# A two-MoE macaron block on one core: the second scatter and the first picks paced by landings, the second half's routing begun ahead of the first pair

## What is computed

```python
x = x + 0.5 * moe(layernorm(x))
x = x + retention(layernorm(x))       # two layers of retention and FFN, 16 heads
x = x + 0.5 * moe(layernorm(x))

def moe(flat):                        # 4096 tokens x 256
    probs = softmax(flat @ router_w + router_bias)      # 16 experts
    top_w, top_i = top_k(probs, 2)
    norm_w = top_w / (sum(top_w) + 1e-6)
    combine = sum(one_hot(top_i, 16) * norm_w)
    routed = combine[:, 15:16] * flat                   # expert 15 passes the token through
    for e in range(15):
        y = silu(flat @ gate_w[e]) * (flat @ up_w[e]) @ down_w[e]     # 256 -> 128 -> 256
        routed = routed + combine[:, e:e + 1] * y
    shared = silu(causal_conv3(flat, conv_w)) * (flat @ shared_up_w) @ shared_down_w
    return shared + routed
```

## Time and profile before

| | us |
|---|---|
| median of three timed runs | 1405.84 |
| lowest and highest | 1404.09, 1406.28 |
| span of the profiled execution | 1579.5 |

### The profile page before, as it was taken

How to read it: one execution, slowest core, us unless ns; L and a number is a source line. 1 busy time by engine, 2 the same in 40 slices (tenths; PEclk the granted TensorE clock), 3 DMA queues, 4 the chain that set the end, 5 groups by cost and what they waited for, 6 DMA issues and landing times.

```text
span 1579.5 us, 30698 instructions
## 1 busy us (share of the span) xinstructions
PE 1351.4 (86%) x11824; PEld 1104.9 (70%) x11824; DVE 1011.0 (64%) x2391; ACT 614.6 (39%) x1034; POOL 571.9 (36%) x460
## 2 busy tenths in 40 slices
PE   6871968876999999999998999999999676496885
PEld 3461968644788888888886888888887446496753
DVE  5661536658977877777768778797787453253623
ACT  5630635422333433343344334424455262263410
POOL 0726033352342323224424443364343704304252
PEclk9975979989999999999999999999999788698998
DMA  9963559650000000000010000000002463355542
GB/s 326 372 213 122 174 175 321 206 190 23 28 2 2 1 2 1 1 2 32 8 58 1 1 15 2 15 15 14 2 28 89 167 229 131 124 181 171 156 150 90
DMA packets 113867, 151.63 MB, mean 96 GB/s; under 512 B 12224, under 2 KB 96192, under 8 KB 113728
## 3 DMA queue, kind: packets, MB, share of 16 engines
q1 hardware_dynamic: 99328, 114.02, 21.8%
q0 software_dynamic: 12288, 33.57, 6.6%
q10 hardware_dynamic: 2112, 2.10, 0.4%
HBM read 78.21 MB, written 71.43 MB: 95 GB/s over the span
## 4 chain that ended last, share of the span: by engine, by line
PE 53%; DVE 16%; another core or an unknown queue 8%; issue 2%; ACT 2%; POOL 0%; DVEq 0%; ACTq 0%
PE l_w_ps L83 8%; PE l_w_ps L85 7%; PE l_w_ps L84 7%; DVE l_probs L2221 4%; PE l_banks L2505 3%; PE l_rm_ps L2537 2%; PE l_banks L83 2%; PE l_banks L84 2%; PE l_banks L85 2%; DVE l_f_lo L2252 2%; PE l_rm_ps L2530 2%; DVE l_full L2174 1%; PE b_gu_ps L83 1%; PE b_t_ps L1284 1%
## 5 line engine op out<-in xcount | busy, mean ns | idle before, releaser
L2221 DVE TENSOR_TENSOR l_probs<-l_banks,l_past 128x512 f32<-128x512 f32 x256 | 160.1, 684 | 29.8 <-PE l_banks L2505 29.7
L1964 ACT ACTIVATE l_act_f<-l_w_ps,l_ffn_b 128x512 f32<-128x512 f32 x120 | 82.7, 690 | 169.0 <-PE l_w_ps L85 163.9
L83 PE MATMUL l_w_ps<-l_w_hi,l_f_hi 128*128 128x256 f32 x496 | 143.6, 290 | 2.6 <-DVE l_f_lo L2252 2.4
L84 PE MATMUL l_w_ps<-l_w_lo,l_f_hi 128*128 128x256 f32 x496 | 139.6, 281 | 0.0
L85 PE MATMUL l_w_ps<-l_w_hi,l_f_lo 128*128 128x256 f32 x496 | 139.5, 281 | 0.0
L2059 POOL TENSOR_TENSOR l_g_lo<-l_q,l_g_hi 128x1024 fp32r<-128x1024 f32 x16 | 39.1, 2447 | 266.9 <-ACT l_g_hi L1955 266.9
L813 POOL DMA_INDIRECT b_picked<-rows,b_pos_i x64 | 61.1, 955 | 137.4 <-DMA rows<-b_yb 88.5
L83 PE MATMUL l_w_ps<-l_b_hi,l_w_hi 128*128 128x512 f32 x240 | 102.2, 426 | 0.3 <-ACT l_f_hi L1965 0.3
L83 PEld LDWEIGHTS l_w_ps<-l_w_hi,l_f_hi 128*128 128x128 f32 x496 | 93.3, 188 | 8.8 <-issue 8.7
L2252 DVE TENSOR_TENSOR l_f_lo<-l_act_f,l_f_hi 128x512 fp32r<-128x512 f32 x128 | 85.9, 703 | 18.5 <-ACT l_f_hi L1965 18.4
L2046 POOL TENSOR_TENSOR l_q_wide<-l_q,l_pair_mask 128x1024 f32<-128x1024 f32 x32 | 60.1, 1899 | 103.7 <-DVE l_q L2189 100.0
(11 more groups left out here) (432 smaller groups left out, 4053.0 us busy)
## 6 DMA issues: line engine op xcount, KB each, us to landing
rows<-a_zeros SPq DMA_DIRECT2D x14, 1024.0 KB, 10.7
a_xb<-rows SPq DMA_DIRECT2D x46, 256.0 KB
rows<-a_yb SPq DMA_DIRECT2D x46, 256.0 KB
b_xb<-rows SPq DMA_DIRECT2D x46, 256.0 KB
rows<-b_yb SPq DMA_DIRECT2D x46, 256.0 KB
a_w_in<-in_moe_w SPq DMA_DIRECT2D x15, 384.0 KB, 10.2
low_dram<-a_w_lo SPq DMA_DIRECT2D x15, 384.0 KB
b_w_lo<-low_dram SPq DMA_DIRECT2D x15, 384.0 KB
```

The source lines that it names most:

```text
L83: tensor.matmul(out, w_hi, x_hi, start=start, stop=False)
L84: tensor.matmul(out, w_hi, x_lo, start=False, stop=False)
L1964: nc.scalar.activation(act_f[:, f, :], hidden_ps(b, f), ACT.Gelu, bias=ffn1_b[:, b.layer, f:f + 1]).then_inc(act_done, 1)
L2221: dve.tensor_tensor(probs[c % 2][:, r * w:(r + 1) * w].rearrange("p (h n) -> p h n", n=P), banks[:, r, :].rearrange("p (h n) -> p h n", n= ...
```

## The change

It is made in four places, in both MoEs:

- In the second scatter, each transfer but the first waits until the one ahead of it has landed. Transfers of pick 0 and pick 1 alternate, so transfer (c, 0) waits for the c-th landing of `scattered[1][1]`, and (c, 1) for the (c+1)-th of `scattered[1][0]`. The first scatter stays as it was.
- In the picks of the first half, a column's first transfer waits until both transfers of the column ahead have landed.
- VectorE takes one step of `rest()` before `low_x(0)` and one before `low_x(1)`, and two steps instead of one after each of pairs 0 and 1.
- TensorE's `count(1)` stands ahead of the first two `turn_x` instead of inside pair 0.

```diff
@@ scatter(b) @@
                 for c in range(PARTS[b]):
                     for k in range(2):
+                        if b == 1 and (c > 0 or k > 0):
+                            pool.wait_ge(scattered[1][1 - k], 16 * (c + k))
                         pool.indirect_dma_start(own_rows[b], bass.IndirectOffsetOnAxis(ap=pos_i[:, b, k, c:c + 1], axis=0),
                                                 normal(START[b] + c), None).then_inc(scattered[b][k], 16)
@@ pick(c) @@
                 for k in range(2):
+                    if b == 0 and c > 0 and k == 0:
+                        pool.wait_ge(picked_in[(c - 1) % PICKED], 32 * ((c - 1) // PICKED + 1))
@@ vector() @@
                 later = rest()
+            next(later)
             low_x(0)
+            next(later)
             low_x(1)
...
                 low_h(n)
-                next(later, None)
+                for _ in range(2 if n < 2 else 1):
+                    next(later, None)
@@ tensor() @@
+            count(1)
             if begins:
                 pe.wait_ge(dve_lo_done, PIECES)
             turn_x(0)
...
                     turn_x(n + 2)
-                if n == 0:
-                    count(1)
```

## The result

| | timed median, us | runs | profiled span, us |
|---|---|---|---|
| before | 1406.06 | 1404.09 to 1407.06 | 1579.5 |
| changed | 1535.48 | 1530.71 to 1540.30 | 1531.5 |

The changed kernel takes 1.0919 times as long, with an interval of 1.0891 to 1.0948: 129 us more, where 67 had been forecast. The span of its profile is shorter than that of the kernel before, and yet its timed runs are longer. In the changed kernel span and time agree within 4 us; it is the profile of the kernel before that stands apart from its times.

A forecast was written before the change was run, and what follows sets the result against it. TensorE bounds the kernel, pairs at 2.89 us unstalled in timed runs; 31.8 + 33.1 (scatters) - 3.1 (already late) + 2.6 (clock) + 1.9 (routing) + 1 (picks) = 67.3 us on 1405.8 gives 1473.1, range 1415 to 1530.

The forecast's parts named there:

- the landing that sets the scatter's period: Second scatter: 2.57 us from issue to woken waiter, 32 transfers in 82.2 us, 31.8 and 33.1 us late.
- the price of the picks: First half's paced picks: 3.82 us a column, the 16th 1 us late in the first MoE, nothing in the second.
- The sign: Whole kernel, timed against the kernel before: slower 0.86, same 0.04, faster 0.10.
- The scatter's starts: Second scatter, from the earlier routing: start at 103.2 us in the first MoE and 1313.4 in the second.
- The 2.3 us of the prediction's estimate: Second scatter: skill's fixed cost and bandwidth give 2.3 us a transfer, 74 us for 32, time about 1456.
- Rival 4: Second scatter and picks: landings as long as the picks' 3.35 us, from shared DMA engines; 1520 to 1545 us, chance 0.09.
- my upper bound: First half's picks: with a landing of 3.35 us a column takes 4.6 us, the 16th 13 and 7 us late.
- 161 us of stalls: Engine stalls during GpSimd's transfer bursts in the profile before, claimed to belong to the profiled execution, not the timed runs.
- the 174 us: Kernel before: profiled span of 1579.5 us over the timed median of 1405.8, claimed to be nearly all profile stalls.
- Rival 1: Scatter and pick bursts: stalls are in timed runs too and pacing removes them; some 36 us faster, 1370, chance 0.10.
- late in its own scatter: Kernel before, second scatter: 1.7 and 1.4 us late in the two MoEs, together 3.1, subtracted from the forecast's sum.
- The late first pair of the second MoE: Second MoE's start: count ahead of the turns delays the first pair by 1.9 us, bounds 0 and 4.

The follow-up runs named there:

- x1: Kernel before plus only the second scatter's waits, each transfer waiting for the landing of the one ahead, both MoEs: 1511.9 us against 1405.3.
- x5: Changed kernel without its wait in the picks; paced second scatter and early routing kept: 1502.9 us, kernel before 1405.6.
- x7: Changed kernel with SP's queue swapped, each turn's store of y ahead of the load of the pair four ahead: 1531.6 us, kernel before 1405.6.
- x2: Kernel before plus only the waits in the picks of the first half: 1437.5 us against 1405.3.
- x6: Changed kernel with the pick wait made real in the second MoE too, adding the count left by the first: 1565.5 us, kernel before 1405.6.
- x3: Kernel before with only the second half's routing begun early, no new waits: 1407.0 us against 1405.3.
- y1: The changed kernel as it is, on a chip where the kernel before takes 1584.5 us: 1611.8 us, ratio 1.0172.
- x4: Kernel before with each second-scatter transfer waiting for the one two ahead, so two in flight: 1437.4 us against 1405.3.
- x8: Kernel before with each second-scatter transfer waiting for the one three ahead, so three in flight: 1416.7 us against 1405.6.
- z1: Kernel before with two second-scatter transfers in flight and the early routing, no pick waits: 1428.0 us against 1405.8.
- z2: Kernel before with three second-scatter transfers in flight and the early routing: 1407.7 us against 1405.8.
- y2: Kernel before with two second-scatter transfers in flight, on a chip where the kernel before takes 1584.5 us: 1538.4 us, ratio 0.9721.
- x9: Kernel before with the low weight parts' stores moved from SP's turns 28 to 42 to 12 to 26: 1576.6 us against 1578.4.
- x12: Kernel before with the first half's picks waiting for the column two back, both MoEs: 1576.1 us against 1578.4.

## Why the prediction was wrong

The forecast was 1473 us within 1415 to 1530; 1535 were measured. Two terms of the sum carry the miss: the landing that sets the scatter's period, and the price of the picks.

**What held.** The sign, and the mechanism: SP waits for the whole second scatter ahead of pair 23's load, the store of y 16 stands behind it, `take_y(18)` waits, then TensorE starts at half clock. x1 and x5 show that this part costs 106.5 us without the early routing and 97.3 with it, x7 that it is this queue order. The scatter's starts were right within 0.7 us against the first gate of their MoE: 5.2 us behind it where 4.5 was forecast, and 4.1 where 4.7 was.

**Mis-sized: the landing.** I took 2.57 us for a scatter's period, from one landing when no pair ran. Quiet, it is 2.67; beside running pairs 2.6 to 5.1. Means of 3.08 and 2.96 over 31 periods make 15.8 and 12.1 us more: 31.8 forecast and 47.4 measured in the first MoE, 33.1 and 43.3 in the second. The row was from the wrong neighbourhood: nearly half of the 32 transfers lie beside loads and stores of 512 KB a pair, and of the landings shown only the store's 3.24 us was taken there. The 2.3 us of the prediction's estimate is under even the quiet 2.67. Rival 4 had this mechanism, and its range of 1520 to 1545 holds the measured time; I gave it 0.09. That its number fits is in part luck. A period of 3.35 puts 25 us more on each scatter and 19 on the picks; measured were 15.6 and 10.2 more on the scatters and 31 on the picks.

**Mis-sized: the picks.** Forecast 1 us, measured 32.2 (x2). A column takes 5.9 us in the first MoE of x2, not 3.82, nor the 4.6 of my upper bound, since what follows the second issue is 3.2 to 6.3 us and not 2.57. In the prediction's own sum, 16 columns of 5.9 us against 60.2 are 34 us late, so the sum's form was right and the landing in it wrong. Against a pair each of 3.27 the head start of 11 us is used up with the fifth column (the first long pair is 32 to 33). Had the wait been real in the second MoE, it would have cost 30 more (x6).

**Missed: the idle wait.** I read the target of the new wait without asking where the semaphore stood at that time.

**Wrong: where the stalls belong.** I put 161 us of stalls down to the profiled execution. That gave the right base for the timed runs shown, which have no stalls, but by luck, for the reason was wrong: x3's profile is unpaced and free of them, and the timed runs of the kernel before on two chips have them. Spans and times agree within 0.8% in every kernel that I ran. So the 174 us are most simply the difference between two sorts of chips: the profile shown of the kernel before would come from one, its times from the other. That is an inference; on which chip either was taken is not known. The rule that I cited from the Trainium skill (NOTIFIC — the notification-queue block, § 7.1) is not borne out as a cause here: no run shows trace records holding an engine. Rival 1, whose stage is a chip with stalls, fails there too: it promised a gain, and y1 is 27 us slower. It had said itself why: above a period of about 2.9 us the wait costs more than the stall, and y1's is 3.02 in the first MoE.

**Small terms.** The kernel before was not 3.1 us late in its own scatter, but some 0.6. x2 has that scatter on a chip of the first sort; gates 19 to 21 are 6.71 us apart there and 6.12 in x3, where it starts early, and in the second MoE 6.10 and 6.17. The late first pair of the second MoE was forecast at 1.9 us; from the last gate of the first MoE to the first of the second it is 971.3 us on average in the four kernels without the early routing (x1, x2, x4, x8) and 973.8 in the seven with it (changed, x3, x5 to x7, z1, z2), 2.5 more. Together that is +1.9, near the +1.7 of x3 (interval -0.4 to +3.9). The lower clock after a gap cost 2.2 us in the first MoE (5.01 against 2.85) and 2.5 in the second, not 1.3.

**The sum as measured.** 47.4 + 43.3 for the gaps, 4.6 for the clock, 33.9 for the picks (88.63 against 54.75 in x3) make 129.2, and 129.4 were measured; the two small terms would add 1.9, which a sum over single profiles cannot tell.

The page on DMA (the Trainium skill, DMA: Bandwidth & Descriptors, § Rules for kernel authors) asks to issue early and wait late. The runs on chips of the first sort agree: waiting for the last transfer, the one two back and the one three back cost 106.5, 32.1 and 11.1 us. On a chip with stalls two in flight gained 46 us (y2), so there the rule does not hold for this burst.

## What to carry to other kernels

A wait between the transfers of a burst costs a landing each, so find what consumes the burst and when, and take the landing from rows with the same traffic beside it. Here three in flight kept about nine tenths of the rate, two about three quarters, one two fifths. When a profile's span and the times differ by a tenth, time and profile the kernel on one and the same chip before calling anything an artefact; and for a semaphore that is reused, ask what it has counted already.

## What the runs showed of the hardware

- Two sorts of chips: the kernel before takes 1405 to 1406 us on three chips of the experiments and 1578 and 1585 on two others, there in 35 and 17 timed runs, none of which was under 1565. All of the difference that I could place lies where GpSimd's indirect transfers are issued back to back. What differs between the chips, and whether it lasts, is open.
- On the second sort, one transfer in flight stalls nothing (8.85 us for three pairs), two little (9.65, then 38.77 for 11 pairs in place of 32.26), and a free burst holds every engine but GpSimd: of 46 to 48 us for three pairs TensorE works 13 (x9), while GpSimd goes on issuing, 32 transfers in 39.9 us. In picks 1.30 us apart on average (x12) the stall is as in a free burst. A scatter with three in flight was not seen there.
- An indirect scatter of 128 rows that is awaited has a period of 2.63 to 2.69 us when the pairs stand (one of 2.81), and up to 5.1 beside their traffic (changed kernel); an awaited column of picks takes 3.1 to 6.7 us from its second issue to the next column there.
- Beside unpaced picks and weight stores the DMA engines moved 347 GB/s at a busy share of 0.95, with the 17 pairs only 5 us slower (x3: 54.75 against 49.81).
